# Grouped attention in a decoder stage: the values' product as three products of split factors, x stored in DRAM during the stage, and one mask moved from ScalarE to TensorE

## The reference

```python
h = rmsnorm(x, ln1_w)
q, k, v = h @ Wq, h @ Wk, h @ Wv            # 32, 4 and 4 heads of 128
q, k = rope(q, pos), rope(k, pos)
k, v = repeat(k, 8), repeat(v, 8)           # each key head serves 8 query heads
s = (q @ k.T) / sqrt(128) + causal_mask     # per sequence and head, 256 x 256
p = softmax(s)
x = residual + (p @ v) @ Wo
```

## Time and profile before

| | us |
|---|---|
| median of 3 runs | 1535.27 (1535.23 to 1543.98) |
| the profiled execution's own time | 1537.94 |
| its span, first to last instruction | 1536.2 |
| TensorE busy in the span | 1342.8 (87%) |
| VectorE busy | 961.9 (63%) |
| ScalarE busy | 792.4 (52%) |
| GpSimd busy | 617.7 (40%) |

### The profile page before, as it was taken

One profiled execution on the slowest core, in us unless ns is written; L12 is line 12 of the kernel. 1 busy time (PEld: TensorE's weight loads), 2 busy tenths in 40 slices (PEclk: granted clock), 3 DMA queues, 4 the chain that ended last, 5 costly groups with the idle time before them and its releaser, 6 DMA issues. The chain is left out here.

```text
span 1536.2 us, 23871 instructions
## 1 busy us (share of the span) xinstructions
PE 1342.8 (87%) x8621; PEld 987.4 (64%) x8621; DVE 961.9 (63%) x1625; ACT 792.4 (52%) x1590; POOL 617.7 (40%) x550
## 2 busy tenths in 40 slices
PE   5788678899799579886789999999999869999998
PEld 4564455644388434433557777776777658888887
DVE  4763754558755587873677777877787554333443
ACT  2455104345532246664567777777877544445442
POOL 5110001101054511211566666666676445555553
PEclk8999779989999678996899999999999979999999
DMA  2000400020000100002000000000000023233231
GB/s 70 1 1 2 121 3 0 4 101 0 1 1 1 38 1 2 2 2 81 7 14 15 15 25 19 15 22 22 15 22 8 8 87 121 96 119 110 105 119 51
DMA packets 29492, 55.58 MB, mean 36 GB/s; under 512 B 6506, under 2 KB 16170, under 8 KB 29204
## 3 DMA queue, kind: packets, MB, share of 16 engines
q1 hardware_dynamic: 29396, 54.30, 11.0%
HBM read 52.98 MB, written 1.21 MB: 35 GB/s over the span
## 5 line engine op out<-in xcount | busy, mean ns | idle before, releaser
L2606 DVE TENSOR_TENSOR e_act<-e_gated,ps 128x512 f32<-128x512 f32 x66 | 45.4, 688 | 158.1 <-POOL e_gated L2411 158.1
L1839 POOL TENSOR_TENSOR a_raw<-a_prod 128x512 f32<-128x512 f32 x72 | 98.3, 1366 | 51.7 <-DVE a_prod L2243 51.7
L1844 POOL TENSOR_TENSOR a_q_low<-a_raw,a_q_high 128x512 fp32r<-128x512 f32 x64 | 82.8, 1294 | 87.2 <-ACT a_q_high L2103 87.2
L2240 DVE TENSOR_TENSOR a_prod<-ps,a_rot 128x512 f32<-128x512 f32 x72 | 49.7, 691 | 93.9 <-PE ps L1888 93.7
L2411 POOL TENSOR_TENSOR e_gated<-e_gate,e_wb 128x512 f32<-128x512 f32 x66 | 85.2, 1292 | 49.8 <-ACT e_gate L2532 44.5
L1848 POOL TENSOR_TENSOR a_o_low<-a_o,a_o_high 128x512 fp32r<-128x512 f32 x64 | 82.9, 1295 | 41.7 <-ACT a_o_high L2154 39.7
L2111 ACT ACTIVATE a_shift<-ident,a_nmax 128x128 bf16<-128x128 f32 x256 | 81.9, 390 | 32.3 <-DVE a_nmax L2252 32.0
L2402 POOL TENSOR_TENSOR e_we_low<-e_we,e_we_high 128x768 fp32r<-128x768 f32 x33 | 60.8, 1842 | 89.5 <-ACT e_we_high L2537 85.5
L1606 DVE SCALAR_TENSOR_TENSOR m_acc<-ps,m_conv_w,m_acc 128x1020 f32<-128x1020 f32 (+2 forms) x60 | 76.0, 1275 | 31.3 <-ACT m_acc L1526 29.9
L1360 PE MATMUL ps<-m_ln_T,m_win 128*128 128x512 f32 x192 | 88.8, 618 | 4.2 <-DMA m_win<-in_m_winT 3.5
L601 DVE TENSOR_REDUCE x_nmax<-ps 128x2 bf16<-128x512 f32 x128 | 82.5, 689 | 11.2 <-PE ps L371 10.9
(11 more groups left out here) (431 smaller groups left out, 4271.2 us busy)
## 6 DMA issues: line engine op xcount, KB each, us to landing
e_wb<-token_weights SPq DMA_DIRECT2D x32, 512.0 KB, 3.9
e_we<-in_experts SPq DMA_DIRECT2D x33, 384.0 KB, 3.1
a_wq<-in_a_wq SPq DMA_DIRECT2D x16, 256.0 KB, 2.7
a_wo<-in_a_wo SPq DMA_DIRECT2D x16, 256.0 KB, 2.8
m_win<-in_m_winT SPq DMA_DIRECT2D x2, 1024.0 KB, 8.8
nf_pickU<-in_nf_pickU SPq DMA_DIRECT2D x2, 768.0 KB
nf_raw<-in_ffn_w SPq DMA_DIRECT2D x3, 352.0 KB
x<-in_x SPq DMA_DIRECT2D x4, 256.0 KB, 6.6
```

Of the source, the lines that this page charges most:

```text
L1839: e.tensor_tensor(raw[:, i % 2, :], prod[:, i % 2, 0, :], prod[:, i % 2, 1, :], ALU.add).then_inc(s_raw, 1)
L1844: e.tensor_tensor(low_part, raw[:, i % 2, :], high_part.bitcast(F32), ALU.subtract).then_inc(s_xl, 1)
```

## The change

Five edits, which hang together by the memory that they take and free:

1. `values` multiplies split factors: `vH`, `vL` for the values and `pH`, `pL` for the probabilities, three products in place of one float32 product for each of the two blocks of keys.
2. The splits for it: `prob_high` on ScalarE (768 columns, L2158 of the new kernel), `prob_low` of the 512 long columns on GpSimd and of the 256 short ones on VectorE (both L1854), `v_low` on VectorE in the prologue (8 instructions).
3. The first pass's long bank gets its mask from a matmul with the identity, as the short bank has it already; `mask_first` goes.
4. Rings and places: `probT` has 3 places, q is kept in 3 halves, `o` splits have 3 places, `raw` lies in `prod` itself, so `rotate(i)` waits for `high` and `low` of piece `i-2` instead of its `add`.
5. `inv`, `invH` and `o` lie where `core.x` was. x is stored in DRAM (`x_saved`, 1 MB) at the start of the stage and loaded back in the next stage, where GpSimd's addition waits for it.

```diff
-        raw = sb("raw", [P, 2, BANK])
-        qH, qL = sb("q_high", [P, 2, 2, T], F32R), sb("q_low", [P, 2, 2, T], F32R)
+        raw = prod[:, :, 0, :]
+        qH, qL = sb("q_high", [P, 3, 2, BANK], F32R), sb("q_low", [P, 3, 2, BANK], F32R)
...
+            e.dma_start(d["x_saved"], core.x[:].rearrange("p t d -> p (t d)")).then_inc(s_saved, 16)
...
+        def prob_low(e, n, part, done):
+            e.wait_ge(s_ph, n + 1)
+            e.tensor_tensor(pL[:, n % 4, part], probT[:, n % 3, part], pH[:, n % 4, part].bitcast(F32),
+                            ALU.subtract).then_inc(done, 1)
...
                 for i in of_step.get(n - 1, ()):
                     low(e, i)
+                if 0 <= n - 1 < N:
+                    prob_low(e, n - 1, slice(0, 2 * S), s_pll)
...
-                e.wait_ge(s_m1, n + 1)
...
-                             start=False, stop=True, skip_group_check=True)
+                             start=(j == 0), stop=False, skip_group_check=True)
+                e.matmul(long[:, :, P:S], ident16[:], two(mask16), start=False, stop=True, skip_group_check=True)
...
             def values(s):
                 p, b = s // B, s % B
                 g = p // 4
+                e.wait_ge(s_pll, s + 1)
+                e.wait_ge(s_pls, s + 1)
...
-                e.matmul(out, v[:, 2 * b, g * P:(g + 1) * P],
-                         probT[:, s % 4, 0:2 * S].rearrange("p (h q) -> p h q", h=2), start=True, stop=False)
...
+                for k, o, part in ((0, out, slice(0, 2 * S)), (1, out[:, :, P:S], slice(2 * S, 3 * S))):
+                    for i, (w, x) in enumerate(((vH, pH), (vH, pL), (vL, pH))):
+                        mm = e.matmul(o, w[:, 2 * b + k, group], heads(x[:, s % 4, part]), start=(k == i == 0),
+                                      stop=(k == 1 and i == 2))
...
+            def prob_high(n):
+                e.wait_ge(s_ex, 2 * n + 2)
+                if n >= 4:
+                    e.wait_ge(s_av, n - 3)
+                e.activation(pH[:, n % 4, :], probT[:, n % 3, :], ACT.Copy).then_inc(s_ph, 1)
...
             def rotate(i):
                 e.wait_ge(s_pc, i + 1)
                 if i >= 2:
-                    e.wait_ge(s_raw, i - 1)
+                    e.wait_ge(s_xh, i - 1)
+                    e.wait_ge(s_xl, i - 1)
...
                 for i in of_step.get(n, ()):
                     rotate(i)
+                if 0 <= n - 1 < N:
+                    prob_low(e, n - 1, slice(2 * S, 3 * S), s_pls)
                 if n % 2 and 0 <= n - 3 < N:
                     split((n - 3) // 2)
...
+            e.dma_start(core.x[:].rearrange("p t d -> p (t d)"), d["x_saved"]).then_inc(s_back, 16)
...
+            e.wait_ge(s_back, 16)
             e.tensor_tensor(core.x[:], core.x[:], res[:], ALU.add).then_inc(s_xr, 1)
```

More of the change, by code:

```diff
@@ L1816, in target @@
             _, p, half, j = what
-            a = slice(half * BANK, (half + 1) * BANK)
-            return qH[:, p % 2, j, a], qL[:, p % 2, j, a], 2 * (B * (p - 2) + 2 * half + 2)
+            at = 2 * p + half
+            return qH[:, at % 3, j, :], qL[:, at % 3, j, :], 2 * (B * ((at - 3) // 2) + 2 * ((at - 3) % 2) + 2)
         def const_low(e, n):
@@ L1970, in scores @@
                 keys = [w[:, g, a:a + P] for w in (kH, kL)]
-                both = [w[:, p % 2, :, a:a + S] for w in (qH, qL)]
+                both = [w[:, at, :, z:z + S] for w in (qH, qL)]
                 e.wait_ge(s_m2, 2 * n + 1)
@@ L1978, in scores @@
                 keys = [w[:, g, a + P:a + S] for w in (kH, kL)]
-                both = [w[:, p % 2, :, a + P:a + S] for w in (qH, qL)]
+                both = [w[:, at, :, z + P:z + S] for w in (qH, qL)]
                 e.wait_ge(s_m2, 2 * n + 2)
@@ L2095, in v_copy @@
                 e.wait_ge(s_v, t + 1)
-                e.activation(v[:, t, :], ps[:, (P2_LONG, AV, SPREAD, OUT)[t % 4], :], ACT.Copy).then_inc(s_vc, 1)
+                e.activation(vH[:, t, :], ps[:, (P2_LONG, AV, SPREAD, OUT)[t % 4], :], ACT.Copy).then_inc(s_vc, 1)
             def high(i):
@@ L2113, in shifts @@
                 ins.then_inc(s_D, 1)
-                if n + 1 < N:
-                    mask_first()
             heads = lambda a: a.rearrange("p (h k) -> p h k", h=2)
             both = lambda a: a[:, None, :].to_broadcast([P, 2, a.shape[-1]])
-            def mask_first():
-                e.activation(heads(ps[:, P1_LONG, :]), both(seed1[:]), ACT.Copy).then_inc(s_m1, 1)
             def mask_second(part):
@@ L2130, in exps @@
                 e.wait_ge(s_p2, 2 * n + 1)
[L2131 to L2133 removed]
+                if n >= 3:
+                    e.wait_ge(s_pll, n - 2)
+                    e.wait_ge(s_pls, n - 2)
+                    e.wait_ge(s_sum, (n - 3) // 2 + 1)
+                e.activation(probT[:, n % 3, 0:2 * S], ps[:, P2_LONG, :], ACT.Exp).then_inc(s_ex, 1)
                 e.wait_ge(s_p2, 2 * n + 2)
[L2135 removed]
+                e.activation(probT[:, n % 3, 2 * S:3 * S], ps[:, P2_SHORT, 0:S], ACT.Exp).then_inc(s_ex, 1)
                 if n + 1 < N:
@@ L2296, in _ @@
             h_low(3)
-            for i in range(1, FIRST):
-                rotate(i)
+            rotate(1)
+            rotate(2)
+            for t in range(4):
+                v_low(t)
+            rotate(3)
+            rotate(4)
+            for t in range(4, 6):
+                v_low(t)
+            rotate(5)
+            for t in range(6, 8):
+                v_low(t)
             for b in range(B):
```

77 lines of the change are left out of this document (42 added, 35 removed).

## The result

After the change the kernel takes 1603.27 us (median of 4 runs, 1599.04 to 1606.58) beside 1536.48 us for the kernel before (4 runs of the same comparison). The ratio is 1.0422, 95% interval 1.0386 to 1.0458: slower. The profiled execution of after took 1599.04 us (span 1597.2, granted clock 0.935). The forecast had 1579 us and a range up to 1600: the direction was right, the size too small by a third.

What follows compares the result with a forecast made beforehand. Bound: the odd steps' chain rotation, split, division, without slack, though TensorE looks full. Plain pairs 20.8 + 1.9, key pairs 19.8, those behind 0.6, prologue 2, end -1.4: +43.7 us, hence 1579 us; range 1543 to 1600.

Steps and rivals of the forecast that it cites:

- end and x's way back: Behind the last rotation, 8 products save 0.24 and 4 masks cost 0.12: -1.4 us; x to DRAM and back: 0.
- plain pairs: 17 pairs of steps without a key piece: 13 x 1.6 = 20.8 us, plus 4 with already blocked splits, 1.9.
- key pairs: Six pairs with an extra key piece, +3.3 us each: odd half 1.5, subtraction 0.8, rotation waiting for POOL's low part 1.0.
- prologue: Eight VectorE subtractions from PSUM ahead of the loop, 5 us, some 3 hidden: +2 us, ends 0 and +5.
- The place with no slack: Odd steps, between rotation and division on VectorE: slack 0.01 us, so whatever is put there is paid in full.
- Odd half: Odd step, 6.29 us before: 7.57 if VectorE's new subtraction gets through and the split is blocked, 8.07 with POOL caught mid-subtraction.
- Even half: Even step, 7.25 us before: 7.13 if VectorE wins the near race with POOL's new subtraction, 7.56 if it waits.
- Mask: One more 256-column matmul on TensorE in front of scores, 0.12 us a step; ScalarE loses 0.52 us.
- Values' product: TensorE's split-factor products in values: 1.05 us instead of 1.29, saving 0.24 us a step.
- (1): Rival: the new VectorE subtraction never meets POOL, pair 13.58 us, kernel 1545 us; chance 0.14.
- (2): Rival: TensorE is the bound after all, values not waiting for the division; 8 us saved, 1527 us; chance 0.06.
- (3): Rival: subtraction and split both blocked fully in every step, or POOL the bound; pair 16.2 us, 1604 us; chance 0.10.

Runs made afterwards that it cites:

- e1_noshort: The kernel after without VectorE's 256-column prob_low (third matmul takes the high factor, its waits go): 1547.91 us, ratio 1.007.
- e3_mask_order: The kernel before with the long bank's mask on TensorE and GpSimd's addition waiting for the odd step's split: 1531.07 us, ratio 0.9982.
- e2_pool: The kernel after with the short subtraction moved to GpSimd, one instruction of 768 columns with the long one: 1552.4 us, ratio 1.0122.
- e2_mask: The kernel before with only the mask of the first pass's long bank moved from ScalarE to TensorE: 1545.44 us, ratio 1.0066.

## Why the prediction was right in direction and short in size

The mechanism held; terms of the sum were too small. In order of what they missed: end and x's way back, -1.4 and 0, measured +4.6 together; plain pairs, 20.8 + 1.9, measured 27.4; key pairs, 19.8, measured 23.4; prologue, 2, measured 4.9. The items give each with its reason.

- *The place with no slack.* Right. The pair grew by 1.91 us where +1.6 was forecast; one 128x256 instruction put ahead of split and division carries it (e1_noshort).
- *Odd half, "7.57 if the subtraction gets through, and 0.5 more (8.07) where POOL is caught".* The dear case was the rule. By rows: 6.29 - 0.24 + 1.13 for the subtraction (1062.29 to 1063.42) + 1.01 for the split (1.41 from start to start instead of 0.40) = 8.19; measured 8.24.
- *Even half, "7.13 or 7.56".* Between: 7.20. The subtraction takes 1.31 from start to start, VectorE's 1.09 of slack is used up. It stays 0.27 under 7.25 - 1.09 + 1.31, since the division is now 0.61 from start to start instead of 0.77 and the residual 0.54 where it took 0.63. "A near race" was none here: GpSimd starts first, by 0.18 us.
- *Plain pairs.* In the 15 that repeat, 24.4 us came up; with the loop's start (3.0) that is 27.4 against 20.8 + 1.9. This is the largest mis-sized term within the loop, mostly by the 0.3 a pair above.
- *Key pairs, 6 x 3.3.* 23.4 instead of 19.8; five are 3.5 to 3.8 longer. The sixth grew by 5.4: TensorE idled 1.71 us for a held split, and then the granted clock was at its lower level, 1.2 GHz, for some 3.4 us (5 x (0.23 + 0.11) / 0.5 from the last two rows), which cost some 1.7:

```profile
966.66 0.51 PE L2020 MATMUL ps<-a_inv_split,a_pick 128*128 128x256 f32 x2 [1.71 <-DVE a_inv_split L2292]
...
960.00:965.00 5.00, 4.95 (x33) 4.07 (x31) 4.08 (x6) 3.93 (x9) 3.90 (x4) 1.00 0.01 3
965.00:970.00 5.00, 3.16 (x11) 2.55 (x12) 3.73 (x6) 2.46 (x7) 2.61 (x2) 0.77 0.00 0
970.00:975.00 5.00, 4.14 (x22) 3.47 (x21) 2.07 (x3) 2.73 (x6) 4.23 (x4) 0.89 0.18 50
```

- *Prologue, "+2, since some 3 of the 5 hide".* +4.9. The cover was no cover: the rotations of pieces 3 and 5 stand behind `v_low`, which waits for ScalarE's copy, and TensorE's pieces follow them. VectorE there:

```profile
737.54 2.48 DVE L2253 TENSOR_TENSOR a_v_low<-ps,a_v_high 128x512 fp32r<-128x512 f32 x4 [3.45 <-ACT a_v_high L2113]
...
747.89 1.29 DVE L2253 TENSOR_TENSOR a_v_low<-ps,a_v_high 128x512 fp32r<-128x512 f32 x2 [3.66 <-ACT a_v_high L2113]
```

- *End, -1.4, and x's way back, 0.* Together +4.6. Behind the last rotation VectorE waits for ScalarE's copy of the probabilities with a division queued behind that wait, a wait the forecast did not look for; and x's load comes late for the residual, with GpSimd idle for it. The load is the smaller part: e1_noshort has the same wait (2.59 us) and a rest of 356.89, 1.2 above before's, so that some 3.5 of the 4.6 go with the short subtraction.

```profile
1247.00 0.42 DVE L1854 TENSOR_TENSOR a_prob_low<-a_probT,a_prob_high 128x256 fp32r<-128x256 f32 x1 [3.27 <-ACT a_prob_high L2158]
...
1259.19 0.43 DVE L1854 TENSOR_TENSOR a_prob_low<-a_probT,a_prob_high 128x256 fp32r<-128x256 f32 x1 [2.75 <-ACT a_prob_high L2158]
```

```profile
1301.36 5.09 POOL L2457 TENSOR_TENSOR x<-x,res 128x2048 f32<-128x2048 f32 x1 [2.25 <-DMA x<-x_saved]
```

- *Mask, 0.12.* Right for the matmul (0.13 in e3_mask_order), wrong for the kernel it was put into alone: there it cost 10 us, 7 of them with ten more held splits, which the forecast did not have as a mechanism.
- *Values' product, 1.05 us instead of 1.29.* Right: 1.06 from its first matmul to the next piece. The saving bought nothing where VectorE sets the step:

```profile
1011.06 0.40 PE L2036 MATMUL ps<-a_prob_high,a_v_high 128*128 128x512 f32 x1
...
1012.12 0.40 PE L1901 MATMUL ps<-a_h_high,a_wq_high 128*128 128x512 f32 x1
```

- *Rivals.* (1) fell: no split gets through. (2) fell: a shorter TensorE gained nothing. (3) was near for the splits but not for GpSimd, which at 54.38 of 70 us was not the bound, and took e2_pool's extra work. Its 1604 us is the time that was measured, but that is luck: it had the pair at 16.2 us, where 15.45 was measured, and 1 us for prologue and end, where 9.5 was.

The sum was 43.7 and the profile has 61.5: loop +8.8, prologue +2.9, end and x +6.0. The medians differ by 66.8; some 5 us of that are between executions.

The rule of the Trainium skill, page "SBUF — State Buffer", section "SBUF: two separate sides": a VectorE operation with two SBUF inputs and a GpSimd one that reads SBUF exclude each other for a whole instruction. The runs agree on the exclusion: of two that stand behind the same rotation, either VectorE takes 0.48 and GpSimd 1.58 us, or GpSimd 1.27 and VectorE 1.60, which then ends 0.28 us after GpSimd. That whichever starts first keeps it is not seen in recorded starts 0.05 us apart, where the first one lost 3 times of 22 in before and 15 of 24 in e2_mask.

## What to carry to other kernels

Price a VectorE operation with two SBUF inputs by where GpSimd is, not by its length: here 0.43 us alone, 1.4 us when held, and another 1.0 us for the next such operation that it pushes into GpSimd's work. Put it where VectorE waits anyway, or give it to GpSimd whole. Where such operations of both engines stand behind the same event, decide the order with a wait; and cut executions at a stage's own start before comparing a few microseconds.
